# A cross-attention kernel on one core: value tile one unit later, shorter prologue and end, half an output tile in column tiles

## The reference

```python
Q = split_heads(x @ Wq.T + bq); K = split_heads(c @ Wk.T + bk); V = split_heads(c @ Wv.T + bv)
scores = einsum('bhqd,bhkd->bhqk', Q, K) / sqrt(32)
attn = softmax(where(mask == 0, -1e9, scores))
out = einsum('bhqk,bhkd->bhqd', attn, V).merge_heads() @ Wo.T + bo
y = out + x
return (y - mean(y)) / sqrt(var(y) + 1e-5) * ln_g + ln_b
```

## Time and profile before

| | before |
|---|---|
| median of 3 runs | 1893.29 us (1891.81 to 1894.22) |
| profiled execution | 1894.68 us, span 1891.7 us |
| TensorE clock granted, mean | 0.976 of full |
| PE busy | 1768.8 us, 94% |
| ACT busy | 1345.3 us, 71% |
| POOL busy | 1302.4 us, 69% |
| DVE busy | 1126.2 us, 60% |
| DMA moved | 164.50 MB |

### The profile page before, as it was taken

The page is one execution under the profiler, slowest core; times in us unless marked ns, Lnnn a source line. Parts: engine busy times, 40 slices in busy tenths (PEclk is TensorE's granted clock), DMA queues, the critical chain, the costliest instruction groups (busy, mean ns, idle before and its releaser), DMA issues.

```text
span 1891.7 us, 34346 instructions
## 1 busy us (share of the span) xinstructions
PE 1768.8 (94%) x12816; PEld 879.7 (47%) x12816; DVE 1126.2 (60%) x2826; ACT 1345.3 (71%) x1537; POOL 1302.4 (69%) x844
## 2 busy tenths in 40 slices
PE   3889999999999999999999999999999999999984
PEld 2535445454544545454454545445454544545431
DVE  2546665656666665666666565666656566665612
ACT  2277786777878677787867778786777878677660
POOL 2074686877778687777868777786877778686574
PEclk9979999999999999999999999999999999999967
DMA  9222232232223223222322322232222223222010
GB/s 317 78 69 70 79 108 75 85 103 75 81 90 108 75 85 103 75 82 89 108 74 85 102 75 85 85 108 75 85 102 75 86 85 108 75 63 80 8 35 33
DMA packets 94020, 164.50 MB, mean 87 GB/s; under 512 B 25888, under 2 KB 34080, under 8 KB 93856
## 3 DMA queue, kind: packets, MB, share of 16 engines
q1 hardware_dynamic: 93856, 162.31, 26.4%
HBM read 140.25 MB, written 22.02 MB: 86 GB/s over the span
## 4 chain that ended last, share of the span: by engine, by line
PE 63%; ACT 11%; POOL 11%; issue 7%; DVE 5%; SPq 1%; DMA 1%; POOLq 0%; ACTq 0%; DVEq 0%
PE proj_bank L772 34%; PE ring L684 16%; POOL total L351 7%; PE ctx_bank L717 6%; ACT probs L445 5%; PE ring L726 4%; DVE ring L543 3%; ACT exp_banks L421 3%; POOL total L359 2%; PE exp_banks L702 2%; ACT q L465 2%; POOL x_lo L338 1%; PE exp_banks L693 1%; SPq L242 1%; ACT c_hi L481 1%
## 5 line engine op out<-in xcount | busy, mean ns | idle before, releaser
L543 DVE CUSTOM_DVE_ANT_0 ring<-ring,bias 128x512 f32<-128x512 f32 x1024 | 688.1, 714 | 457.4 <-PE ring L684 456.3
L445 ACT ACTIVATE probs<-exp_banks 128x1024 f32<-128x1024 f32 x512 | 523.0, 1022 | 227.5 <-PE exp_banks L702 227.5
L421 ACT CAST exp_banks<-biasT 128x1024 f32<-128x1024 bf16 x512 | 520.6, 1017 | 23.2
L684 PE MATMUL ring<-k,q 32*128 32x512 f32 x3072 | 498.2, 427 | 23.8 <-ACT exp_banks L421 13.1
L693 PE MATMUL exp_banks<-q,k 32*128 32x512 f32 x3072 | 501.6, 431 | 5.4 <-ACT exp_banks L421 5.4
L684 PEld LDWEIGHTS ring<-k,q 32*128 32x128 f32 x3072 | 251.1, 184 | 284.3 <-DVE maxes L543 149.7
L351 POOL TENSOR_TENSOR total<-probs 128x2048 f32<-128x2048 f32 x64 | 293.1, 4580 | 82.6 <-ACT probs L445 82.6
L351 POOL TENSOR_TENSOR total<-total,probs 128x2048 f32<-128x2048 f32 x64 | 293.6, 4587 | 81.2 <-ACT probs L445 79.0
L359 POOL TENSOR_TENSOR total<-total,probs 128x1024 f32<-128x1024 f32 x128 | 304.0, 2397 | 11.2 <-ACT probs L445 4.2
L717 PE MATMUL ctx_bank<-probs,v 128*32 128x512 f32 x2048 | 282.3, 624 | 0.9 <-DVE ctxT L598 0.8
L772 PE MATMUL proj_bank<-wo,ctxT 128*128 128x512 f32 x512 | 254.7, 621 | 8.4 <-DVE rows L564 4.5
(11 more groups left out here) (69 smaller groups left out, 2061.7 us busy)
## 6 DMA issues: line engine op xcount, KB each, us to landing
w_tile<-w_scratch SPq DMA_DIRECT2D x128, 512.0 KB, 3.6
raw<-cT_dram SPq DMA_DIRECT2D x64, 256.0 KB, 4.7
raw<-xT_dram SPq DMA_DIRECT2D x64, 256.0 KB, 4.5
raw<-mask_dram SPq DMA_DIRECT2D x64, 256.0 KB, 2.8
rows<-x_dram SPq DMA_DIRECT2D x64, 256.0 KB, 3.2
out_dram<-rows SPq DMA_DIRECT2D x64, 256.0 KB, 2.1
w_scratch<-k SPq DMA_DIRECT2D x8, 256.0 KB, 6.0
max_rows<-max_scratch SPq DMA_DIRECT2D x128, 8.0 KB
```

The source lines that it names most:

```text
L421: nc.scalar.copy(exp_banks[:, 2 - 2 * wave:4 - 2 * wave, :], biasT[:, kc:kc + 1, :].to_broadcast([P, 2, L])).then_inc(seeded, 1)
L445: nc.scalar.activation(probs[:, u % PS, 2 - 2 * wave:4 - 2 * wave, :], exp_banks[:, 2 - 2 * wave:4 - 2 * wave, :], ACT.Exp).then_inc(exps, 1)
L543: nc.vector.tensor_tensor_reduce(out=ring[:, n % 2], in0=ring[:, n % 2], in1=bias[:, c], scale=1.0, scalar=LOWEST, op0=ALU.subtract, op1=A ...
L684: mm = nc.tensor.matmul(ring[:, (n + h % 2) % 2], q[rows_h, g % QS, a, c * P:(c + 1) * P], k[rows_h, g % KS, b, :], start=part == 0, stop= ...
```

## The change

- In SLOT, V tile 1 goes from unit 12 to 13 and K tile 2 from 13 to 12. The last mask block goes from unit 0 to 1 (MASKS).
- Half 0 of an O tile is made as four matmuls of 32 output rows each, in four column tiles, for each of its two parts; half 1 stays as it was.
- VectorE widens and normalises right behind the inversion, in the same step, and no longer behind two row maxima of the next.
- Three slots for the weights of Q and K tiles (WS). The first three tiles' weights are split straight into them; the rest of Wq and Wk is split in steps -7 and -6 and written to DRAM in two DMAs each. Loads are issued in another order, and waits at the start of the engines go.
- The bias product and the writing of the banks move into steps -6 to -3.
- END is UNITS + 2. The last group's sums are made by TensorE from `probs` behind each context group. The last four output tiles are made full size, one in each of the four score banks; GpSimd adds the bias to the residual rows ahead, and VectorE scales and shifts.

The second transpose and the multiplication have gone ahead of the two maxima. The diff, cut to its core:

```diff
-END = UNITS + 20
-KS, QS, PS, CS, RAW = 4, 3, 4, 6, 8
+END = UNITS + 2
+LAST = GROUPS - 1
+KS, QS, PS, CS, RAW, WS = 4, 3, 4, 6, 8, 3
...
-            12: ("V", 1, 1), 13: ("K", 1, 2), 14: ("V", 1, 2), 15: ("Q", 1, 2)}
+            12: ("K", 1, 2), 13: ("V", 1, 1), 14: ("V", 1, 2), 15: ("Q", 1, 2)}
...
+    MASKS = {13: 0, 14: 1, 15: 2, 1: 3}
...
             def load_weights(tile):
                 i = PLAN.qk[tile]
-                if i >= 2:
-                    sp.wait_ge(proj_done, PLAN.no[PLAN.qk_list[i - 2]] + 1)
+                if i >= WS:
+                    sp.wait_ge(proj_done, PLAN.no[PLAN.qk_list[i - WS]] + 1)
                 else:
-                    sp.wait_ge(wk_scratch if tile[0] == "K" else wq_scratch, 2 * NG * FULL)
+                    return
+                sp.wait_ge(wk_scratch if tile[0] == "K" else wq_scratch, 2 * FULL)
...
+            load_weight(WkT, probs[:, 0], wk_loaded)
             for t in range(NK):
                 load_raw(0, 0, t)
+            load_weight(WqT, probs[:, 1], wq_loaded)
             for t in range(NK):
                 load_raw(0, 1, t)
...
+            for dst, src in ((bk_s, bk), (bq_s, bq)):
+                sp.dma_start(dst[:, :], src).then_inc(qk_bias_loaded, FULL)
+            load_weight(WvT, probs[:, 2], wv_loaded)
+            load_weight(WoT, wo[:, :, :], wo_loaded)
...
+                if y == -8:
+                    scratch(1, (total[:, :, :], rows[:, :, :]), wq_split, wq_scratch)
+                if y == -7:
+                    scratch(0, (ctxT[:, 0:NG], probs[:, 3]), wk_split, wk_scratch)
...
+            def prologue(y):
+                if y == -7:
+                    split(wq_raw, by_tile(total[:, :, :]), by_tile(rows[:, :, :]), wq_split)
+                if y == -6:
+                    split(wk_raw, by_tile(ctxT[:, 0:NG]), by_tile(probs[:, 3]), wk_split)
+                    dve.wait_ge(consts_loaded, 4 * FULL)
+                    nc.vector.tensor_copy(recipT[:, :, :], bv_s[:, :].unsqueeze(2).to_broadcast(
+                        [P, NG, P])).then_inc(bv_wide, 1)
...
             for y in range(START, END):
-                g, at = divmod(y - 5, NC)
-                summed = g if at == 0 and 0 <= g < GROUPS else None
+                prologue(y)
                 row_max(y, 0)
                 row_max(y, 1)
                 if PLAN.max_group(y) is not None:
                     turn_max(PLAN.max_group(y))
-                if summed is not None:
-                    widen_recip(summed)
-                    normalise_ctx(summed)
...
                 if PLAN.sums(y):
                     turn_sums(PLAN.sums(y)[1])
                     invert_sums(PLAN.sums(y)[1])
+                    widen_recip(PLAN.sums(y)[1])
+                    normalise_ctx(PLAN.sums(y)[1])
...
+            def finish_last(n):
+                tile, m = ("O", NB - 1, n), PLAN.o["O", NB - 1, n]
+                dve.wait_ge(tail_done, n + 1)
+                dve.wait_ge(tail_biased, n + 1)
+                nc.vector.tensor_tensor(rows[:, n], exp_banks[:, n], rows[:, n],
+                                        ALU.add).then_inc(o_out, 1)
+                row_statistics(tile)
+                row_aggregate(tile)
...
+            def sum_last(u):
+                n = PLAN.ring["S", LAST]
+                if u % NC == 0:
+                    pe.wait_ge(ring_free, n - 1)
+                for h in range(HG):
+                    mm = nc.tensor.matmul(ring[h * D:(h + 1) * D, n % 2], ones[:, :],
+                                          probs[:, u % PS, h], start=u % NC == 0,
+                                          stop=u % NC == NC - 1)
...
+                    if kind == "O" and half == 0:
+                        for d in range(0, P, D):
+                            nc.tensor.matmul(proj_bank[d:d + D, 0], a[:, d:d + D], b, start=m == 0,
+                                             stop=False)
+                        continue
...
+            for n in range(NC):
+                for t in range(NK):
+                    if n == 0 and t == 0:
+                        pe.wait_ge(exps, 2 * UNITS)
+                        pe.wait_ge(normed, LAST)
+                    if n == 0 and t == NK - 1:
+                        pe.wait_ge(normed, GROUPS)
+                    mm = nc.tensor.matmul(exp_banks[:, n],
+                                          ctxT[:, (GROUPS - NG + t) % CS, n * P:(n + 1) * P],
+                                          wo[:, t], start=t == 0, stop=t == NK - 1)
+                mm.then_inc(tail_done, 1)
```

More of the change, by code:

```diff
@@ L86, in mask @@
     def mask(self, y):
-        s, kc = divmod(y + 3, UPS)
-        return ("M", s, kc) if kc < NC and 0 <= s < NB else None
+        s, kc = (y + 3) // UPS, self.MASKS.get(y % UPS)
+        return ("M", s, kc) if kc is not None and 0 <= s < NB else None
     def casts(self, y, when):
@@ L217, in _, with load_weight @@
         def _(sp):
[L218 to L219 removed]
+            def load_weight(w, dst, done):
                 sp.dma_start(dst, w.rearrange("(t p) n -> p t n", p=P)).then_inc(done, FULL)
[L221 to L223 removed]
             def load_raw(seq, use, t):
@@ L312, in _ @@
                     store_row(tile)
+                if y == UNITS - 2:
+                    for n in range(NC - 1):
+                        load_row(("O", NB - 1, n))
+            load_row(("O", NB - 1, NC - 1))
+            for n in range(NC):
+                store_row(("O", NB - 1, n))
             for n in range(NC):
@@ L410, in _ @@
                     scale_row(tile)
+            for n in range(NC):
+                m = PLAN.o["O", NB - 1, n]
+                pool.wait_ge(bo_ready, 1)
+                pool.wait_ge(rows_loaded[n], FULL * (m // NC + 1))
+                nc.gpsimd.tensor_tensor(rows[:, n], rows[:, n], bo_all[:, :],
+                                        ALU.add).then_inc(tail_biased, 1)
+            for n in range(NC):
+                inverse_deviation(("O", NB - 1, n))
         @block.scalar
@@ L437, in exp @@
                 act.wait_ge(scored, u + 1)
+                if u == PS - 1 and wave == 0:
+                    act.wait_ge(wk_scratch, 2 * FULL)
                 if u >= PS and wave == 0:
@@ L648, in _ @@
+            for n in range(NC):
+                finish_last(n)
+                if n:
+                    scale_last(n - 1)
+            scale_last(NC - 1)
         @block.tensor
         def _(pe):
-            pe.wait_ge(wo_loaded, FULL)
-            pe.wait_ge(bv_wide, 1)
-            for t in range(NK):
-                mm = nc.tensor.matmul(proj_bank[:, 0], recipT[:, t], wo[:, t], start=t == 0,
-                                      stop=t == NK - 1)
-            mm.then_inc(bv_wo, 1)
-            for b in range(HG):
-                mm = nc.tensor.matmul(exp_banks[:, b], wo[:, 0, 0:P], wo[:, 0], start=True, stop=True)
@@ L658, in _, with prologue @@
-            mm.then_inc(bv_wo, 1)
-            pe.wait_ge(bo_ready, 1)
-            pe.wait_ge(consts_made, 8)
-            pe.wait_ge(w_split, 7)
+            pe.wait_ge(consts_made, 8)
+            def prologue(y):
+                if y == -6:
+                    pe.wait_ge(wv_split, 2)
+                    for b in range(HG):
+                        mm = nc.tensor.matmul(exp_banks[:, b], wv_hi[:, 0, 0:P], wv_hi[:, 0],
+                                              start=True, stop=True)
+                    mm.then_inc(banks_written, 1)
+                if y == -5:
+                    pe.wait_ge(wo_loaded, FULL)
+                    pe.wait_ge(bv_wide, 1)
+                    for t in range(NK):
+                        mm = nc.tensor.matmul(ctx_bank[:, 0], recipT[:, t], wo[:, t], start=t == 0,
+                                              stop=t == NK - 1)
+                    mm.then_inc(bv_wo, 1)
@@ L710, in context @@
                 pe.wait_ge(exps, 2 * u + 2)
-                if kc == 0 and g >= 1:
-                    pe.wait_ge(normed, g)
+                if kc == 0:
+                    pe.wait_ge(*((normed, g) if g else (bo_ready, 1)))
                 if g % NG == 0:
```

135 lines of the change are left out of this document (84 added, 51 removed).

## The result

The changed kernel takes 1827.59 us (median of four runs, 1827.31 to 1830.59); the kernel before, in the same rounds, 1892.55 (1891.16 to 1894.22). The ratio is 0.966, with a 95% interval of 0.9643 to 0.9677. The prediction was 1826, range 1812 to 1846.

A forecast was written before the change was run, and what follows sets the result against it. TensorE was taken to set the pace. From 1891.7 us, 12.9 (prologue), 33.0 (steady part) and 21 (end) came off, leaving a span of 1824.8; with time around the span and the median's offset, 1826.4. Predicted 1826, range 1812 to 1846.

The forecast's parts named there:

- Value tile and masks: Units 13, 14, 15, 0 and 1: reordered work saves 1.84 us a sequence, 27.6 us over 15.
- Column tiles: First halves of output tiles: 0.20 us saved each, only units 2 and 4 counted in most sequences; 6.6 us together.
- rival B: GpSimd's stretch before unit 8's sums shortens too, all 0.95 a sequence counts: 8.3 us more saved, 1818; 12%.
- Rival C: Output tiles: column tiles bring nothing because leaving them costs more; 6.6 us less saved, 1833; 14%.
- F: Half output tiles: four column tiles reading the same wo columns take turns; 300 us slower, over 2100; 4%.
- VectorE's order: Sums: widening and normalising ahead of the next unit's maxima lose 0.08 us a sequence, 1.2 us in all.
- Rival E: Sums: VectorE's moved operations are fully late, 0.3 to 0.5 at 64 sums; 19 to 32 us less saved; 5%.
- GpSimd as unit 8's limit: Unit 8: takes near 8.25 us, with GpSimd's sums as releaser of TensorE's sums.
- Prologue: Start: first scores at 33.3 us instead of 49.15, second at 42.3 instead of 54.33; 12.9 us saved, ends 6 and 19.
- End: Last group: sums on TensorE and output tiles in four banks without waits save 21 us, ends 14 and 24.
- rival D: Prologue or end give half, by a later mask or low clock: 10 to 17 us less saved, 1836 to 1843; 14%.

The follow-up runs named there:

- experiment 1: Kernel before with only the swap of value tile 1 and K tile 2 between units 12 and 13: 1877.66 us, ratio 0.9916.
- experiment 12: Changed kernel with value tile 1 back in unit 12 and K tile 2 back in unit 13: 1847.22 us, ratio 0.9756.
- experiment 5: Changed kernel with ScalarE's last casts in unit 4, GpSimd's last splits in unit 5, and no column tiles: 1830.33 us, ratio 0.9667.
- experiment 4: Changed kernel with ScalarE's last two casts moved from unit 5 to 4 and GpSimd's last splits from 6 to 5: 1819.66 us, ratio 0.9609.
- experiment 6: Changed kernel with VectorE widening and normalising behind two row maxima again, last group excepted: 1825.89 us, ratio 0.9645.
- experiment 9: Changed kernel with ScalarE's mask conversions one step later in the first sequence: 1826.53 us, ratio 0.9647.
- experiment 2: Changed kernel with full matmuls again for the first halves of output tiles in units 5 and 6: 1828.80 us, ratio 0.966.
- experiment 10: Changed kernel with early mask conversions one step later and VectorE's split of Wv behind K tile 0's finish: 1824.50 us, ratio 0.9635.

## Why the prediction was right

The time was 1.6 us above the forecast, the span (1825.4) 0.6 above its sum. By its steps:

- **Value tile and masks.** 1.84 us a sequence predicted. The means of units 13, 14, 15, 0 and 1 add up to 35.16 before and 33.33 after: 1.83. Experiments 1 and 12 give the swap 1.23 to 1.36 of it. The mask gives the rest: unit 0 falls from 8.12 to 7.47 and unit 1 rises from 6.24 to 6.41, with the swap undone too.
- **Column tiles.** 0.20 a half tile predicted; units 2 and 4 gave 0.21 and 0.20, experiment 5 against 4 gave 0.20. That units 5 and 6 count for nothing held, and rival B fell: units 5, 6 and 8 together took 21.56 before and 21.55 after. Rival C (nothing gained) and F (four tiles that stream one operand take turns) fell: a half tile took 1.83 us.
- **VectorE's order.** 0.08 a sequence lost was predicted, 0.10 gained measured (experiment 6). The step that failed is the late maximum behind the sums of unit 8. It did come late: the second maximum is done 4.99 us behind the start of the sums, at 1003.32, where it had been 4.77. That is 0.22 and not up to 0.3, and the slack covered all of it: the next scores start at 1003.41, 5.08 behind the sums as before. Behind the other sums of a sequence no scores came later for it either. What was gained, in unit 13 above all, the forecast had not looked for. Rival E fell with it.
- **GpSimd as unit 8's limit.** 8.25 predicted, 8.22 measured, and experiment 4 showed that an earlier chain shortens it. But the forecast saw one chain where there are two: VectorE's ends 0.53 us sooner than GpSimd's in the changed kernel, and in the kernel before, where GpSimd was read as the only releaser, the two ended almost together. For the forecast it made no difference, since GpSimd's was the longer one behind the change.
- **Prologue.** 12.9 predicted, 11.9 measured. K tile 0 was to start at 12.4 and started at 14.98, 2.6 late: the casts by ScalarE began at 8.21, behind a table load, and GpSimd's four low parts took 5.92 us (4.94 before). Only 1.1 us of that reached Q tile 0 (25.36 against 24.3), since the K copy was late as predicted. The late copy was laid to the mask alone; experiment 9 showed Wv's split beside it. By the second scores 0.5 us of the miss were left (42.80 against 42.3). The other 0.5 lie behind them: 0.9 had been counted there for unit 0's mask, and from the second scores to the first context it takes 40.43 us instead of 40.82, 0.4 less. Even this needed the better clock: experiments 2 and 6, with the same prologue, reached the first context at 86.3, 8.8 us ahead of the kernel before and not 11.9. No run put the old prologue back, so this part is read from traces alone.
- **End.** 21 predicted for the last sequence and what follows, 20.5 measured, as a balance of terms that were off. The matmuls ran at the high clock from the first (14.1 us, not 15.4); the chain behind the last one took 8.5 instead of 7.8; the sums were 3.9 sooner instead of 3. Against these stand 2.2 us more in the last sequence. The added sums, which the forecast had called free, are not what made them: 1.9 of the 2.2 were lost before the first added sum (from the context of unit 0 to that of the last group it takes 79.97 us before and 81.88 in the changed kernel). What differs there is the clock: in the 20 us from 30 us behind the start of that sequence it was 0.94 before, 0.86 in the changed kernel and 1.00 in experiment 9, which took 78.21.

So rival D (prologue or end give half) did not come, though the low clock that it named was there in part, in the last sequence. Where the sum is nearer than its parts, that is luck: the misses were +1.0, -0.8 (steady part, first sequence included) and +0.5, and the clock of a single execution moves the first and the last of them by about 3 us each.

## What to carry to other kernels

Compare each repeating step with its neighbour that does the same work: two steps that differed by 1.1 us at equal work led to an edit worth 20 us. Before you count a saving, go back from the next wait on another engine; what lies inside that engine's chain counts only when the chain is shortened too, and behind it there may be a second one, here 0.5 us away. Where two waits end within hundredths of each other, look for another run in which they lie apart. Where a kernel's runs differ by 3 us, price a small edit by the repeating part of the trace, not by the median.

## What the runs showed of the hardware

**The granted clock moves between executions of the same instructions.** With the same prologue the first context started at 83.2 us in the changed kernel and at 86.3 in experiment 2, though scores just ahead of 55 us started within 0.1 of each other (54.20 and 54.30). TensorE between 60 and 83 us, in the changed kernel and in experiment 2:

```profile
60.00:83.00 23.00, 20.20 (x135) 1.00 0.14 48
```

```profile
60.00:83.00 23.00, 20.23 (x110) 0.85 0.15 48
```

The same again in the last sequence (experiment 9), which took 91.6 to 95.2 us in the kernels with the sums by TensorE. Each of the two is worth about 3 us, as much as the runs of most kernels here differ. The Trainium skill, "TensorE: Matmul & The Clock Gate", section "Part 1: The HAM clock gate", says of a kernel's start that the point at which the same kernel warms up varies from run to run. These traces show such a variation later: from 34 to 60 us the clock was 0.99 or 1.00 in the changed kernel and all of its variants, and it differed only behind that. In the start of experiment 10, TensorE kept the high clock behind 1.65 us without work; in the changed kernel it was at the low one behind 5.27.

**VectorE and GpSimd slow each other.** A 128x512 cast from and to SBUF took VectorE 0.43 us alone (6.21) and 1.38 beside GpSimd's splits (13.74); a two-operand operation 0.69 and 1.64. GpSimd's four low parts of the context and of x took 5.92 and 6.24, against 4.94 and 4.98 in the start of the kernel before, where VectorE had nothing to do beside them. In proportion the smallest pay most: at the end the 128x1 operations of the deviation, beside VectorE, took 0.54 and 1.01 us instead of 0.19 and 0.55, for every row block but the first. The Trainium skill, "GPSIMD Engine Reference", section "1. Specifications", says that the two share their SBUF interfaces, and that operations of VectorE with two SBUF inputs or in a two-port mode contend; the rows agree.

**What a change from column tiles costs.** A context group takes 0.996 us before a full tile and 0.883 before column tiles; half an output tile behind it takes 1.915 as full tiles and 1.830 as column tiles. Four column tiles that read the same 512 columns of one operand ran no slower than four with different ones: 0.43 us from round to round in the half output tile, 0.45 in the context group.
